# Dynamic filters: the Newton step by chunk through the PSUM bank of the gelu's input, two of the pair adds moved from GpSimd to TensorE

## What is computed

```python
h = x
for _ in range(STEPS):                                   # 5 steps
    t = gelu(einsum('oc,bchw->bohw', W1, h) + b1)
    k = einsum('oc,bchw->bohw', W2, t) + b2              # 64 * 9 channels
    k = k.reshape(B, C, KE, H, W)
    k = k / (norm(k, axis=2, keepdims=True) + EPS)       # EPS = 1e-6
    p = patches(h)                                       # the 9 shifted copies of h
    y = sum(p * k, axis=2)
    h = h + alpha * y
# the layer's result, added to the layer's input before its group norm, is the output
```

## Time and profile before

| | us |
|---|---|
| median of three runs | 20135.72 |
| the profiled execution, whole | 20080.48 |
| its span | 20078.7 |
| dynamic filters, first to last instruction (15564 to 20078.7) | 4514 |

### The profile page before, as it was taken

How to read it: one execution, slowest core, us unless ns; L and a number is a source line. 1 busy time by engine, 2 the same in 40 slices (tenths; PEclk the granted TensorE clock), 3 DMA queues, 4 the chain that set the end, 5 groups by cost and what they waited for, 6 DMA issues and landing times. The chain is left out here.

```text
span 20078.7 us, 217701 instructions
## 1 busy us (share of the span) xinstructions
PE 12353.6 (62%) x73490; PEld 6114.7 (30%) x73490; DVE 10535.6 (52%) x14652; ACT 5526.4 (28%) x7765; POOL 9453.1 (47%) x8026
## 2 busy tenths in 40 slices
PE   5553699999999202333333333333358899999998
PEld 2551366666666101111111111111112333333332
DVE  4557544444444333443443444344422788888887
ACT  1114333333333000000000000000010666666666
POOL 0113100000000106886887788688800787878787
PEclk9999856656666556666666666666679999999999
DMA  4104222222222494335334433533342112121201
GB/s 94 33 21 102 55 38 36 37 38 36 36 37 38 135 195 111 95 95 131 95 95 107 120 95 95 131 96 95 95 86 58 33 22 42 21 42 22 42 19 30
DMA packets 1399772, 1408.47 MB, mean 70 GB/s; under 512 B 771709, under 2 KB 1116045, under 8 KB 1383565
## 3 DMA queue, kind: packets, MB, share of 16 engines
q1 hardware_dynamic: 1106892, 742.84, 18.5%
q0 software_dynamic: 221184, 604.27, 10.4%
q10 hardware_dynamic: 70976, 50.83, 0.8%
HBM read 1036.74 MB, written 276.84 MB: 65 GB/s over the span
## 5 line engine op out<-in xcount | busy, mean ns | idle before, releaser
L1359 POOL DMA_INDIRECT dc_g<-corners,dc_idx x4608 | 5253.7, 1140 | 1326.0 <-issue 1260.9
L1954 POOL TENSOR_TENSOR df_sq<-df_sq 128x512 f32<-128x512 f32 x1920 | 2713.0, 1427 | 1866.6 <-ACT df_sq L1902 1839.5
L1432 PE MATMUL dc_ps<-ident,dc_s 128*128 128x128 f32 x2560 | 674.0, 428 | 4296.9 <-DVE dc_s L1523 4294.8
L1079 POOL TENSOR_TENSOR nz_vp<-nz_vp,nz_den 128x2048 f32<-128x2048 f32 x16 | 105.8, 6610 | 4814.7 <-DMA nz_den<-den_d 4814.7
L1515 DVE TENSOR_TENSOR dc_g<-dc_g,dc_wt 128x2304 f32<-128x2304 f32 x512 | 1308.6, 2556 | 2001.0 <-DMA dc_g<-corners,dc_idx 2000.9
L1902 ACT ACTIVATE df_sq<-df_pk,vecs 128x512 f32<-128x512 f32 x2880 | 1921.1, 685 | 1326.0 <-DVE df_pr L2056 1309.2
L2056 DVE SCALAR_TENSOR_TENSOR df_pr<-df_pk,vecs,df_h 128x512 f32<-128x512 f32 x2880 | 2047.6, 741 | 407.1 <-PE df_pk L1840 264.5
L1432 PEld LDWEIGHTS dc_ps<-ident,dc_s 128*128 128x128 f32 x2560 | 472.0, 218 | 4480.6 <-DVE dc_s L1523 3352.1
L1392 ACT ACTIVATE dc_st<-dc_ps 128x512 f32<-128x512 f32 x640 | 327.0, 607 | 4934.2 <-PE dc_ps L1432 4934.2
L1840 PE MATMUL df_pk<-df_t,df_wp 64*128 64x512 f32 x3840 | 1389.8, 642 | 364.7 <-ACT df_sq L1902 302.1
L916 DVE TENSOR_REDUCE at_mx<-at_pt 128x4 f32<-128x512 f32 x1024 | 707.8, 691 | 1605.4 <-PE at_pt L779 1605.4
(11 more groups left out here) (271 smaller groups left out, 19428.1 us busy)
## 6 DMA issues: line engine op xcount, KB each, us to landing
df_h<-df_h SPq DMA_DIRECT2D x160, 512.0 KB, 7.1
dc_g<-corners,dc_idx POOLq DMA_INDIRECT x4608, 2.8
corners<-dc_xt SPq DMA_DIRECT2D x16, 4160.0 KB, 41.5
dc_xp<-x SPq DMA_DIRECT2D x8, 4096.0 KB, 40.8
cv_xp<-x SPq DMA_DIRECT2D x8, 4096.0 KB, 50.0
y<-sp_p SPq DMA_DIRECT2D x128, 192.0 KB, 2.8
y<-sp_p SPq DMA_DIRECT2D x64, 384.0 KB, 4.3
at_a<-y SPq DMA_DIRECT2D x64, 384.0 KB
```

The costliest lines, as they stand in the source:

```text
L1359: nc.gpsimd.indirect_dma_start(gt[:, r, k, :, :].rearrange("p a c -> p (a c)"), None, image, bass.IndirectOffsetOnAxis(ap=idx[:, s, r, k:k ...
L1432: i = nc.tensor.transpose(ps[:, j, 128 * r:128 * r + 128], sm[:, r % 2, 128 * j:128 * j + 128], env.ident[:, :])
L1954: nc.gpsimd.tensor_tensor(a, a, sq[:, (KK * n + other) % RING, :], ALU.add).then_inc(nadded, 1)
```

## The change

- GpSimd keeps the adds 0+2 and 1+3 of the squares and 6+7, 6+8; the adds 0+4 and 1+5 are gone. TensorE sums the square tiles 4 and 5 by a further pair of matmuls, ahead of the pair over 0 and 1, in one accumulation. All four lie in one row.
- The Newton step goes by chunk: behind products 0, 1, 2 and 3 of chunk n VectorE runs `check`, `refine`, `update` and (last step) `residual` of chunk n-6 (LAG = 6). `scale` on GpSimd stands once per chunk, for chunk n-5, behind its first two adds.
- `check` writes its result to the PSUM bank `df_p1` instead of `df_n`. `refine` reads and writes that bank, and `update` reads it. The bank is also that of the gelu's input: `check` of chunk n-6 waits for the gelu of chunk n and for the update of chunk n-7, and `hid` of chunk n+1 waits for the update of chunk n-6.
- The last step's stores and loads of `df_raw` go by chunk, with a semaphore per buffer. The first four chunks of `df_raw` are loaded at the layer's start. Copies of the next image's rows come at other places in SyncE's list.

```diff
-    BANKS, RING = 5, 15
+    BANKS, RING, LAG, ADDS = 5, 15, 6, 4
...
+        def wait_update(eng, n):
+            b, step, g = GROUPS[n // CH]
+            if step < STEPS - 1:
+                eng.wait_ge(moved, CH * updates(b, step + 1, g) - CH + n % CH + 1)
+            else:
+                eng.wait_ge(stepout, CH * (b * GR + g) + n % CH + 1)
...
-                else:
+                    continue
+                for i in range(CH):
+                    o = CH * (b * GR + g) + i
+                    store(o)
+                    if o + CH < CH * B * GR:
+                        load_raw(o + CH)
+                    if i == 1 and g and b + 1 < B:
+                        sp.wait_ge(normed, (b + 1) * GR + g)
+                        copy(g - 1)
+                if b + 1 < B:
                     sp.wait_ge(stepout, CH * (b * GR + g + 1))
...
                 if n:
                     pe.wait_ge(active, n)
+                if n >= LAG + 1:
+                    wait_update(pe, n - LAG - 1)
...
-                pe.wait_ge(nadded, 6 * n + 4)
+                pe.wait_ge(squared, KK * n + 6)
                 if n:
                     pe.wait_ge(njoined, n)
-                for s in range(2):
-                    last = nc.tensor.matmul(pn[64 * s:64 * s + 64, :], pair[:, :], sq[:, (KK * n + s) % RING, :], start=True, stop=True,
+                for k in (4, 5, 0, 1):
+                    s = k % 2
+                    if k == 0:
+                        pe.wait_ge(nadded, ADDS * n + 2)
+                    last = nc.tensor.matmul(pn[64 * s:64 * s + 64, :], pair[:, :], sq[:, (KK * n + k) % RING, :], start=(k >= 4), stop=(k < 4),
...
-                add(n, 0, 4, 1)
-                add(n, 1, 5, 2)
-                if q and c == 2:
-                    scale(q - 1, 2)
+                if n >= LAG - 1:
+                    scale(n - LAG + 1)
...
+                dve.wait_ge(active, min(n + LAG + 1, NC))
+                if n:
+                    wait_update(dve, n - 1)
+                nc.vector.scalar_tensor_tensor(out=p1[:, :], in0=nr[:, q % 2, i, :], scalar=env.vecs[:, V_EPS:V_EPS + 1], in1=inv[:, i, :],
...
+                nc.vector.scalar_tensor_tensor(out=p1[:, :], in0=p1[:, :], scalar=-2.0, in1=yr[:, n // CH % 2, n % CH, :],
...
+                    nc.vector.scalar_tensor_tensor(out=centre(n), in0=rows(p1[:, :]), scalar=alpha[:, 0:1], in1=centre(n),
...
-                    if q >= 2 and c == 0 and k < CH:
-                        update(q - 2, k)
-                    if q >= 2 and c == 0 and 4 <= k < 4 + CH and GROUPS[q - 2][1] == STEPS - 1:
-                        residual(q - 2, k - 4)
+                    if n >= LAG and k < 4:
+                        (check, refine, update, residual)[k](n - LAG)
```

More of the change, by code:

```diff
@@ L1798, in _ @@
                 copy(g)
+            for o in range(CH):
+                load_raw(o)
             for b, step, g in GROUPS:
-                if step == STEPS - 2 and g == 0:
-                    load_raw(b, 0)
                 if step < STEPS - 1:
@@ L1967, in _ @@
             for n in range(NC):
[L1968 removed]
                 add(n, 0, 2)
                 add(n, 1, 3)
[L1971 to L1976 removed]
+                if n >= LAG - 1:
+                    scale(n - LAG + 1)
                 singles(n)
                 add(n, 6, 7)
[L1979 to L1985, removed]
+                add(n, 6, 8, 3)
+            for n in range(NC - LAG + 1, NC):
+                scale(n)
         @block.vector
@@ L2007, in check, with refine @@
                                                op0=ALU.add, op1=ALU.mult).then_inc(checked, 1)
[L2009 to L2018, removed]
+            def refine(n):
+                dve.wait_ge(checked, n + 1)
+                dve.wait_ge(scaled, n + 1)
+                nc.vector.scalar_tensor_tensor(out=p1[:, :], in0=p1[:, :], scalar=-2.0, in1=yr[:, n // CH % 2, n % CH, :],
+                                               op0=ALU.add, op1=ALU.mult).then_inc(refined, 1)
@@ L2019, in update @@
+            def update(n):
+                b, step, g = GROUPS[n // CH]
                 dve.wait_ge(refined, n + 1)
-                y = rows(yr[:, q % 2, i, :])
                 if step < STEPS - 1:
-                    nc.vector.scalar_tensor_tensor(out=centre(n), in0=y, scalar=alpha[:, 0:1], in1=centre(n), op0=ALU.mult, op1=ALU.add
-                                                   ).then_inc(moved, 1)
+                    nc.vector.scalar_tensor_tensor(out=centre(n), in0=rows(p1[:, :]), scalar=alpha[:, 0:1], in1=centre(n),
+                                                   op0=ALU.mult, op1=ALU.add).then_inc(moved, 1)
@@ L2024, in update @@
                 else:
-                    o = CH * (b * GR + g) + i
+                    o = CH * (b * GR + g) + n % CH
                     if o >= CH:
[L2027 to L2036, removed]
@@ L2038, in _, with residual @@
-            CHECK = {(1, 6): 0, (1, 8): 1, (2, 1): 2, (2, 3): 3}
-            REFINE = {(2, 5): 0, (2, 7): 1, (3, 1): 2, (3, 3): 3}
+                        dve.wait_ge(stored[o % CH], 32 * (o // CH))
+                    nc.vector.scalar_tensor_tensor(out=rows(yo[:, o % CH, :]), in0=rows(p1[:, :]), scalar=alpha[:, 0:1], in1=centre(n),
+                                                   op0=ALU.mult, op1=ALU.add).then_inc(stepout, 1)
+            def residual(n):
+                b, step, g = GROUPS[n // CH]
+                if step == STEPS - 1:
+                    o = CH * (b * GR + g) + n % CH
+                    dve.wait_ge(raw_in[o % CH], 32 * (o // CH + 1))
+                    dve.wait_ge(stepout, o + 1)
+                    nc.vector.tensor_tensor(yo[:, o % CH, :], yo[:, o % CH, :], ro[:, o % CH, :], ALU.add).then_inc(o_out, 1)
```

66 lines of the change are left out of this document (29 added, 37 removed).

## The result

The kernel after takes 20159.3 us (median of 20 runs, 20143.8 to 20172.4), the kernel before 20130.0 measured beside it (20 runs, 20108.1 to 20145.4). The ratio is 1.0015, 95% interval 1.0008 to 1.0022: a difference within 0.2%, on the slower side. The forecast was 20140, 4 us above the kernel before; measured are 29.

What follows compares the result with a forecast made beforehand. The prediction took TensorE's own work plus a bank chain of product, square and tap as the bound. Body +18.5, head +3.4 and tail -18 gave +4 us on 20135.7, so 20140 us, range 20090 to 20220.

Steps and rivals of the forecast that it cites:

- What bounds the kernel: Whole layer: TensorE's own work plus a bank chain of product, square, tap, which VectorE's Newton work can lengthen; GpSimd in neither.
- The added pair: TensorE's row in every chunk: 0.86 us more, not absorbed by the bank chain; floor from 11.95 to 12.81 us.
- hidden pair: Rival, three chunks a group: bank chain shrinks by what the pair adds; -201 us, 19939 us; chance 0.09.
- VectorE's relief: Each chunk: VectorE has about 10 us of work in 12.8 and keeps up, so the stretches fall to TensorE's floor.
- Roots' stretch: Table load to first tap after the gelu: stays 16.21 us; slow clock costs 0 to 1.63 a group, taken as 0.41.
- slow clock in most groups: Rival, roots' stretch: half clock falls on the path; +95 us if full in each group, 20235 us; chance 0.22.
- Clock stays high: Rival, roots' stretch: fuller TensorE row avoids the drop to half clock; -32 us, 20108 us; chance 0.11.
- Residuals: Last-step groups: one residual lies in each chunk within VectorE's spare 2 us, so all 36.8 us go.
- New waits: Shared bank, GpSimd's scale, image loads and row copies: all new waits priced at 0.
- Head and tail: Before the first table load +3.4 us; at the end fewer chunks and a smaller store, -18 us (-15 to -21).
- Sum: Whole kernel: body +18.5, head +3.4, tail -18 make +4 us; median 20140 us, with 55 us carried over.
- the forecast's case: Whole kernel lands between 20100 and 20185 us, relief and added pair nearly cancelling; chance 0.53.

Runs made afterwards that it cites:

- e1: Changed kernel without the added pair of square matmuls, GpSimd's two adds back, Newton step still by chunk: ratio 0.9889 to the kernel before, layer 4292.0 us.
- e3: Changed kernel with check, refine and update in place in SBUF, no waits on the shared PSUM bank: ratio 1.0010 to the kernel before, layer 4537.4 us.
- e5: Changed kernel with extra matmuls, their results overwritten, in TensorE's pauses behind the roots: ratio 0.9984 to the kernel before, layer 4484.4 us.
- e4: Changed kernel without the added pair, six adds on GpSimd, Newton step by chunk but in place in SBUF: ratio 0.9893 to the kernel before, layer 4296.0 us.
- e2: Kernel before with only the added pair, two adds moved from GpSimd to TensorE: ratio 1.0096 to the kernel before, layer 4713.8 us.
- e8: Kernel before with only extra overwritten matmuls in TensorE's pauses behind the roots: ratio 0.9989 to the kernel before, layer 4476.6 us.
- e7: Kernel before with the added pair and extra overwritten matmuls in TensorE's pauses behind the roots: ratio 1.0005 to the kernel before, layer 4525.8 us.
- e9: Changed kernel without the added pair, overwritten matmuls behind the roots and ahead of the taps that wait for the gelu: ratio 0.9886, layer 4280.0 us.
- e6: Changed kernel without the added pair, overwritten matmuls only in TensorE's pauses behind the roots: ratio 0.9907 to the kernel before, layer 4319.8 us.
- e10: Changed kernel without the added pair, sums of products moved behind tap 3, sum of squares behind tap 5: ratio 0.9891 to the kernel before, layer 4284.5 us.

## Why the prediction was right, point by point

**What bounds the kernel.** Right. TensorE's row sets the distance: e1 takes exactly the pair off it, and GpSimd's two adds come back free of charge.

**The added pair: 0.86 a chunk, not hidden.** Right to 0.02 us in every stretch (12.80 and 12.83 for 12.81; 9.68 for 9.68), and e1 confirms the 201 us. The rival of a hidden pair is out.

**VectorE's relief.** Right as a result: the stretches are at TensorE's floor. `update` took 0.735 and `check` 1.24, as priced, `refine` 0.68 for 0.74. By the rule of the Trainium skill (SBUF — State Buffer, "SBUF: two separate sides") `refine` with one PSUM operand should no longer wait for GpSimd, and `check` should. The trace agrees: 680 to 699 ns for the one, 750 to 1862 for the other. e3 shows that it doesn't matter.

**Roots' stretch.** T to the first tap is 16.20 in the plain group, as forecast. **This term held the one error of size.** I took 0.41 us a group for the slow clock; it was 0.66 (34 groups of 78, 1.52 us each), 51.6 us instead of 32. Its basis was wrong in two ways. I wrote that the slow clock comes *late* in some groups; the windows show that it comes sooner and lasts twice as long, here and in the group of the earlier trace rows:

```profile
17427.96 1.83 PE L1840 MATMUL df_pk<-df_t,df_wp 64*128 64x512 f32 x2 [0.40 <-ACT df_sq L1902]
17429.72 5.39 PE L1851 MATMUL df_py<-df_pr,df_pair 128*64 128x512 f32 x12
...
17428.20:17430.20 2.00, 2.00 (x4) 0.35 (x5) 0.52 (x2) 1.99 (x2) 0.00 (x0) 0.51 1.24 196
```

The clock is at 0.51 there from T + 4.8, where in the plain group of the earlier trace rows it fell at T + 5.7, and the `sums` take 5.39 us instead of 4.49. And I scaled the mean of 0.34 that was already paid, though my own text had the better way: 29 of 78 distances before carry it (19 plain ones at 55.6 instead of 54.7, 10 with residuals at 58.3 instead of 57.4). The pair takes away the slack in front of the gelu, so each pays nearly the full 1.63 that I had worked out as the worst: 29 x 1.63 / 78 = 0.61. S1 stands at T + 21.70 in the long group above, against the 21.71 of the prediction. What grew was the price in each group, from 0.9 to 1.55, hardly their number, 29 to 33. Nor did the time at 1.2 GHz grow: in the 78 groups it was 389 us before and is 379 after. The rival "slow clock in most groups" was priced for 78 of them; 33 paid.

**Clock stays high.** Not so in the changed kernel. e5 forces it and gets 52 us, where the rival had 32, the mis-sized term again.

**Residuals.** Right: all of their 36.8 us went. A group with one in each chunk runs from T 16617.08 to 16672.47, 55.39, though a residual took 1.39 us in mid-layer and not 0.67; the time that VectorE has to spare took it.

**New waits at 0.** Right; e3 and e4 are without the waits on the shared bank and are no shorter; no run takes out the others by themselves.

**Head and tail.** +4.0 for +3.4, and -20.0 for -18. The last four chunks took 20146.61 to 20161.3, 3.7 us each, for 3.6.

**Sum.** Body +38.2 for +18.5, of which 51.6 - 32.0 = 19.6 is the clock term; the layer +22.2 for +4. The medians moved by 29; the 7 us beyond the layer are inside what the stages ahead of it scatter. The 55 us by which the profiled execution lay below the median before did not carry over (after, it lies 7.5 above), but they cancel in a comparison of medians. So the forecast's case held (20100 to 20185), in its upper half.

**What the prediction didn't look for.** It priced the two halves of the change only together. Apart, they are -222 us (e1) and +199.5 us (e2) in the layer. They don't add up to the +22 of both together. With fillers, which take out most of the slow clock, the pair costs 49 us on the old order (e8 to e7) and 204 on the new (e9 to e5): in the old order VectorE's Newton work already held up two of the stretches (12.61 and 11.98 in the earlier trace rows) and covered most of the pair. The first can be followed in the rows: 78 x (54.74 - 52.8) = 151, residuals 37, slow clock 14, ends 20, together 222. The sentence "the relief of VectorE and the added pair nearly cancel" was right, and was where to ask whether the second half is needed. It isn't: GpSimd wasn't the bound, and e1, e4 and e9 beat the kernel before by 1.1% and the changed one by 1.2 to 1.3%.

## What to carry to other kernels

When a change gives one engine relief and another more work, price the halves apart, and ask of the relieved engine whether anyone ever waits for it; here the adds cost nothing where they were, and 201 us as matmuls on the bounding engine. A stall that another wait covers is not free once the cover is used up: count the groups in which it occurs and charge each the uncovered price, instead of scaling the mean that was paid so far. Before an order is turned around, add up the bounding engine's own row without its waits, since that sum is the most that the new order can reach.

## What the runs showed of the hardware

The granted clock fell to 1.2 GHz behind pauses of TensorE of about 2 us inside a row that is otherwise full: 1.73 + 0.40 us ahead of the `sums` (after), 2.23 (e6), 2.32 (e8), 2.98 (e10) ahead of the taps. Such a pause did not always bring it down: in e6 it did in 48 groups of 78. Behind the 1.37 or 1.38 us of e5 and e7 the taps ran at full clock, 3.94. In the kernel after, the same pauses were followed by 3.4 us at 1.2 GHz in 45 groups and by 6.8 in 33; the long ones began sooner, and why was not found. The Trainium skill (TensorE: Matmul & The Clock Gate, "What's actually happening") has the drop after idling and the return after work, and the rows agree with both. What I hadn't expected is its price here, 52 us in the layer after and some 185 in e2, and that useless matmuls in the pause win it back.
